# Two reciprocal roots on another engine, a load ahead of a store, and statistics behind low parts, in an attention and mixture-of-experts layer

## Time and profile before

| | |
|---|---|
| median of 3 runs | 2802.78 us (2802.04 to 2803.43) |
| the profiled execution, its own time | 2804.82 us |
| its span | 2803.1 us |
| TensorE busy | 2755.0 us, 98% of the span |
| VectorE busy | 2185.9 us, 78% |
| ScalarE busy | 1405.3 us, 50% |
| GpSimd busy | 637.9 us, 23% |
| mean granted clock of TensorE | 0.988 of full speed |
| on the chain that ended last | TensorE 89%, VectorE 4%, transfers 3% |

### The profile page before, as it was taken

How to read it: one execution, slowest core, us unless ns; L and a number is a source line. 1 busy time by engine, 2 the same in 40 slices (tenths; PEclk the granted TensorE clock), 3 DMA queues, 4 the chain that set the end, 5 groups by cost and what they waited for, 6 DMA issues and landing times.

```text
span 2803.1 us, 41819 instructions
## 1 busy us (share of the span) xinstructions
PE 2755.0 (98%) x13088; PEld 2287.4 (82%) x13088; DVE 2185.9 (78%) x3194; ACT 1405.3 (50%) x2495; POOL 637.9 (23%) x627
## 2 busy tenths in 40 slices
PE   8999999999999999999999999999999999999988
PEld 7888888888888888888888888888887878888867
DVE  5888888888888888888888888888888777433346
ACT  5555555566555555755555556555555321244424
POOL 2121211122222122221111213221211100266510
PEclk9999999999999999999999999999999889999999
DMA  3111111113111111221111113111110411478943
GB/s 117 38 35 38 34 37 34 34 34 116 34 37 35 34 34 38 64 84 37 34 34 34 34 36 110 34 37 34 34 42 27 138 48 41 136 229 252 246 135 138
DMA packets 209640, 193.53 MB, mean 69 GB/s; under 512 B 14620, under 2 KB 162076, under 8 KB 209552
## 3 DMA queue, kind: packets, MB, share of 16 engines
q1 hardware_dynamic: 199056, 180.47, 20.4%
q0 software_dynamic: 10496, 12.02, 2.2%
HBM read 166.41 MB, written 36.18 MB: 72 GB/s over the span
## 4 chain that ended last, share of the span: by engine, by line
PE 89%; DVE 4%; DMA 3%; issue 2%; ACT 1%; POOL 1%; SPq 0%; POOLq 0%; ACTq 0%; DVEq 0%
PE banks L1718 36%; PE banks L1733 24%; PE banks L1756 12%; PE banks L1640 4%; PE banks L1689 3%; PE banks L1649 3%; DMA acc_rows<-rows_b,who 2%; PE banks L1702 2%; PE banks L1743 2%; PE banks L1571 1%; DVE colsum L1277 0%; POOL acc_rows L686 0%; PE banks L1676 0%; PE banks L1596 0%; DVE neg_max L1262 0%
## 5 line engine op out<-in xcount | busy, mean ns | idle before, releaser
L1718 PE MATMUL banks<-xt,w_sb 128*128 (+1 forms) x4608 | 1108.6, 390 | 6.6 <-DVE xt L1356 6.5
L906 ACT ACTIVATE rows_a<-banks,neg_max 128x1024 f32<-128x1024 f32 x512 | 572.5, 1118 | 893.2 <-DVE neg_max L1262 892.8
L1718 PEld LDWEIGHTS banks<-xt,w_sb 128*128 128x128 f32 x4608 | 866.3, 188 | 187.2 <-POOL w_sb L625 6.5
L1262 DVE TENSOR_REDUCE neg_max<-banks 128x1 f32<-128x1024 f32 x512 | 626.0, 1223 | 285.9 <-PE banks L1733 283.1
L1733 PE MATMUL banks<-qk 128*128 128x512 f32 x3072 | 781.0, 390 | 3.2 <-ACT rows_a L906 3.0
L1733 PEld LDWEIGHTS banks<-qk 128*128 128x128 f32 x3072 | 576.9, 188 | 124.8 <-issue 3.4
L1277 DVE SCALAR_TENSOR_TENSOR colsum<-rows_a,inv,colsum 128x1024 f32<-128x1024 f32 x448 | 586.3, 1309 | 18.8 <-DVE inv L1269 1.5
L625 POOL TENSOR_TENSOR w_sb<-raws,w_sb 128x512 fp32r<-128x512 f32 x192 | 258.0, 1344 | 1201.6 <-ACT w_sb L860 1201.6
L1756 PE MATMUL banks<-wo_sb,val 128*128 128x512 f32 x1536 | 372.0, 391 | 1.2 <-DVE y_sb L1312 1.2
L1756 PEld LDWEIGHTS banks<-wo_sb,val 128*128 128x128 f32 x1536 | 285.9, 188 | 67.8 <-DVE y_sb L1312 8.0
L1640 PE MATMUL banks<-xt 128*128 128x512 f32 x768 | 194.7, 413 | 0.0
(11 more groups left out here) (184 smaller groups left out, 2262.5 us busy)
## 6 DMA issues: line engine op xcount, KB each, us to landing
raws<-in_w_qkv SPq DMA_DIRECT2D x192, 256.0 KB, 2.9
wo_raw<-in_w_o SPq DMA_DIRECT2D x64, 256.0 KB, 2.8
y_sb<-in_x SPq DMA_DIRECT2D x32, 256.0 KB, 4.2
raw_own<-in_w_gate SPq DMA_DIRECT2D x16, 512.0 KB
raw_own<-in_w_up SPq DMA_DIRECT2D x16, 512.0 KB
raw_own<-in_w_down SPq DMA_DIRECT2D x16, 512.0 KB
raws<-in_xT SPq DMA_DIRECT2D x25, 256.0 KB, 3.0
x_wide<-y_sb SPq DMA_DIRECT2D x24, 256.0 KB, 3.7
```

Source lines behind the costliest of these rows:

```text
L906: act.activation(ex[:, t % 2], p_s[:, t % 2], ACT.Exp, bias=neg_max[:, t % 2], accum_out=rowsum[:, t % 2]).then_inc(act_e, 1)
L1262: dve.tensor_reduce(neg_max[:, t % 2], p_s[:, t % 2], AX_X, ALU.max, negate=True)\
L1718: ins = pe.matmul(p_g[:, g % 2], w_sb[:, a, r, c], xt_part(batch_par, b, c, half * NB, NB), start=(c == 0 and (a, b) == PASSES[0]), stop=( ...
```

## The change

Three edits. The scale and shift of turns 6 and 7 are computed on GpSimd, by the `scale_x` that is there for the others; for turn 6 in front of three iotas, for turn 7 behind the store of turn 1's weights. `load_rows(5)` and its wait stand in front of `store_x(7)` on SyncE. `stats_o(0)` stands behind `lo_t(3, 0)` and `lo_t(3, 1)` on VectorE.

```diff
--- before.py
+++ after.py
@@ -576,9 +576,9 @@
         store_a(0)
         sp.wait_ge(out_a[2], 16)
         load_rows(4)
-        store_x(7)
         sp.wait_ge(pe_t, TT * 4)
         load_rows(5)
+        store_x(7)
         store_a(2)
         store_a(4)
         sp.wait_ge(out_a[2], 32)
@@ -713,6 +713,7 @@
             pool.wait_ge(act_s, 2 + h)
             pool.tensor_tensor(s_down[:, LO, two], s_raw[:, two], rounded(s_down[:, HI, two]),
                                ALU.subtract).then_inc(pool_s, 1)
+        scale_x(6)
         pool.iota(iota_s[:], [[1, C_SLOTS]], base=0, channel_multiplier=0,
                   allow_small_or_imprecise_dtypes=True).then_inc(pool_k, 1)
         pool.iota(names[:, :, 0], [[0, TURNS * TT * TOPK]], base=1, channel_multiplier=1,
@@ -723,6 +724,8 @@
         for c in range(TURNS):
             on_pool.wait_ge(dve_w, 2 * c + 2)
             pool.dma_start(rows_of(weights_of, c), dense[:, c % 2]).then_inc(out_w[c % 2], 16)
+            if c == 1:
+                scale_x(7)
 
         pool.wait_ge(pe_t, TT * 6)
         for q in range(2):
@@ -1081,12 +1084,6 @@
         tt, ts, stt = dve.tensor_tensor, dve.tensor_scalar, dve.scalar_tensor_tensor
         ro = Chain(dve, ro_c)
         link = Chain(dve, ln_c)
-
-        def scale_x(c):
-            on_dve.wait_ge(act_q, 2 * TT * (c + 1))
-            on_dve.wait_ge(act_ln, TT * (c - 1))
-            ln_rsqrt(dve, link, EPS, n_square[:, c % 2], small[:, 0], n_scale[:, c % 2], small[:, 2], 1.0 / D)
-            tt(n_shift[:, c % 2], n_mean[:, c % 2], n_scale[:, c % 2], ALU.mult).then_inc(scaled, 1)
 
         def stats_o(c, tiles=range(TT)):
             q, i = OUT_BUF[c], OUT_ORDER.index(c)
@@ -1390,7 +1387,6 @@
         choose_experts(0)
         lo_t(2, 2)
         lo_t(2, 3)
-        scale_x(6)
         weigh(0)
         choose_groups(1)
         add_shared(0, 0)
@@ -1429,8 +1425,6 @@
             for j in range(TT):
                 add_shared(u, j)
             collect(u)
-            if u == 2:
-                scale_x(7)
 
         add_logits(6)
         choose_groups(6)
@@ -1488,10 +1482,10 @@
             lo_hidden(n, f)
 
         share_step(5, 0)
-        stats_o(0)
         share_step(5, 1)
         lo_t(3, 0, True)
         lo_t(3, 1, True)
+        stats_o(0)
         share_step(5, 2)
         stats_o(2)
         share_step(5, 3)
```

## The result

| | kernel before | changed kernel |
|---|---|---|
| median of the first runs | 2802.41 us (4 runs, 2795.53 to 2803.43) | 2781.76 us (4 runs, 2779.92 to 2782.15) |
| its profiled execution | 2804.82 us | 2782.15 us |
| its span | 2803.1 us | 2780.4 us |
| mean granted clock | 0.988 | 0.992 |
| TensorE busy | 2755.0 us | 2746.6 us |

The ratio is 0.993, with a 95% interval of 0.9913 to 0.9947: faster, by 20.6 us (0.7%). The forecast was 2786.4 us, range 2782.8 to 2793.2, so the time came out 4.6 us under the forecast and 1.0 us under the range. The direction was right, the number was not.

The account below looks back on a forecast made before the run. TensorE, busy 98% of the span, was taken as the bound. Terms 0 + 0 + 5.7 + 0.9 + 9.8 = 16.4 us off 2804.8 gave 2788.4 for such an execution, 2786.4 us for the median; range 2782.8 to 2793.2.

Parts of the forecast that it names:

- Load ahead of the store: Routing, turn 5: TensorE's 3.72 us wait for rows_a and the low clock behind it go; 5.7 us gained (5.2 to 6.4).
- the clock: Routing, behind logits: the shift may remove or bring a clock drop; 0.9 us gained, bounds 4.4 gained to 2.7 lost.
- a drop that the forecast had among its bounds: Routing, behind turn 5's logits: a low clock may newly come there, costing 2.7 us.
- The drop behind turn 6's logits: Routing: product takes 8.28 us at clock 0.65 against 5.56 at full; a third of the 2.7 us taken as gain, 0.9.
- Roots: Scale and shift of turns 6 and 7 moved from VectorE to GpSimd: each worth 0 us.
- Statistics behind low parts: End of kernel: TensorE's 9.40 us wait goes, 12.2 us removed, 2.3 and 0.15 back; net 9.8 us (8.1 to 10.2).
- The new wait of 2.3 us before `down(5)`: End: down(5) would wait for the low part of part 2, still behind stats_o(0); 2.3 us lost.
- A low clock inside `down(5)`: End: clock drop after the new 2.3 us wait, about 1.7 us lost; none taken in the forecast.
- Neither moves against the other: End: load of accumulated rows and TensorE's work keep their spacing, so stats_o(0) still ends at 2702.09, where the next product starts.
- Swallowed: Rival: accumulating transfers paced by memory, so 5.7 and 0.9 us are lost, 2793.0 us; chance 0.15, including load still late.
- Locked out: Rival: VectorE's two-input SBUF instructions stretch GpSimd's root beyond 25 us; 2805 us, slower than before; chance 0.02.
- the forecast's limit: Routing, turn 7: the root may end until about 25 us after ScalarE's sums (2257.5) without cost.

Follow-up runs that it names:

- the four unmoved rows: Profiles of four kernels with stats_o(0) where it was, first load of accumulated rows about 11 us behind gate_up(5, 0): lengths 119.6, 120.3, 120.3, 120.0 us.
- before_delay: Kernel before plus 24 small dependent GpSimd products in front of the last pair of accumulating transfers: 2799.46 us (10 runs), ratio 1.0000.
- later: Changed kernel with stats_o(0) moved behind share_step(5, 2) and stats_o(2) behind share_step(5, 3): 2780.53 us (7 runs), ratio 0.9951 to the kernel before.
- load_only: Kernel before with only load_rows(5) and its wait put in front of store_x(7): 2791.25 us (11 runs), ratio 0.9975.
- roots_only: Kernel before with only the two roots (turns 6 and 7) moved to GpSimd: 2791.12 us (12 runs), ratio 0.9979.
- load_tail: Kernel before with the load ahead of the store and the statistics behind the low parts, both roots left on VectorE: 2779.75 us (6 runs), ratio 0.9944.
- after_again: The changed kernel, unchanged, timed again in a job with the kernel before: 2782.32 us (11 runs), ratio 0.9948.
- after_delay: Changed kernel plus 24 small dependent GpSimd products in front of the last pair of accumulating transfers: 2786.74 us (5 runs), ratio 0.9961 to the kernel before.
- the two kernels with the delay: Changed kernel with 24 GpSimd products ahead of the last accumulating transfers, 2786.74 us; the same with both statistics one place further down, 2782.51 us.

## Why the prediction was wrong

**The step that failed: "2804.8 - 16.4 = 2788.4 for such an execution, 2786.4 for the median".** The 16.4 is not the part that failed. The changed kernel is at 2781.9 as the median of its 15 runs, the kernel before at 2798.3 as the median of its 106 runs in the five jobs: 16.4 apart, or 15.2 (10.6 to 18.7, from the interval of the ratio) within the one job that has both. That it agrees to a tenth is luck: the interval is 8 us wide, and several terms behind it were off in both directions, as shown below. What did not hold is the 2802.8 it was taken from. Its three runs lay within 1.4 us of each other and were read as the kernel's time; of the 106 only 13 are over 2802.0, and they reach from 2786.4 to 2805.9. With 2798.3 in its place, 4.5 us less, the same sum gives 2781.9. The range was built from the terms of the change alone and held nothing for the base.

**The profile of before was one execution of many, too.** Against that of after it differs by 22.7 us, because three things fell badly in it and better in the other: the low clock in turn 1's logits (2.9 us, in front of the edits), the expert stage (2.0 us) and the late transfers (lag 14.8 against 11.0). The last is 4.2 us by the lengths 124.3 and 120.1, the latter the mean of the four unmoved rows with a lag near 11. Without the three, 13.6 of the 22.7 are left. The expert stage takes 248.9 to 252.4 us in the profiles without a delay of the transfers, in no order of the edits. Turn 1's logits take 6.87 or 6.88 us in eleven of the 19 profiles and 3.66 to 3.94 in eight. Both occur where the edits in front of them are the same (before 6.88 and before_delay 3.85; `later` 6.87 and after 3.94), so an edit is not needed for it. Seven of the eight, however, are among the ten with both roots on GpSimd; whether these make the short time more frequent stays open.

**Load ahead of the store, 5.7, and the clock, 0.9.** Together 6.6; the starts of the experts differ by 5.6 on average, and the load alone is worth 7.0 in time. The wait is gone in every profile with this edit or the root of turn 7, and the product behind it runs at full clock. But the price was that of one execution: of the five profiles that have the wait, two (3.72 and 3.40 us) show the low clock behind it, with transposes of 1.97 us, and three (1.66 to 1.93 us) do not:

```profile
2294.55 1.09 PE L1571 MATMUL banks<-ident,rows_a 128*128 128x128 f32 x8 [1.66 <-DMA rows_a<-x_wide]
```

In these three less than 2 us hang on the load, not 6.4. What makes up the rest of load_only's 7.0 us (4.2 to 10.1) no run here shows. VectorE limits the gain as forecast where the clock in front of turn 6's second pair of transposes is full. TensorE then waits for the low part, in load_only:

```profile
2317.41 1.23 PE L1571 MATMUL banks<-ident,y_sb 128*128 128x128 f32 x8 [0.27 <-DVE xt L1122]
```

Seven of the fourteen profiles without the wait for rows_a have this, 0.26 to 0.36 us. The other seven, the changed kernel's two among them, have a low clock behind turn 5's logits in its place, a drop that the forecast had among its bounds and the profile of before did not show:

```profile
2307.53 1.95 PE L1565 MATMUL banks<-ident,y_sb 128*128 128x128 f32 x8
```

From turn 5's transposes to that second pair of turn 6 it is 26.21 us there and 25.14 in load_only, so the drop costs about 1.1 us here. The drop behind turn 6's logits, taken as a third gone, is still there in the changed kernel (7.74 us for 8.28). In time the term of the clock cannot be told from chance; starts differ by up to 8.3 us among profiles with the wait and by 8.6 among those without.

**Roots, 0 and 0.** Right in the sum, wrong in the reason. The forecast brought `write_x(7)` from 2284.34 to about 2273.4 (measured: 2268.74, and 2272.60 in roots_only), and stopped there. Behind it in SyncE's order stands store_x(7), and behind that the load TensorE waits for. So the root of turn 7 alone is worth 6.2 us (1.1 to 8.4). In the whole change no worth of it shows, since the load no longer stands behind that store (load_tail against the changed kernel). Whether the root of turn 6 is worth anything by itself stays open.

**Statistics behind low parts, 9.8.** By the lengths: 124.3 (forecast from) to 116.5, 115.9 or 114.6 with a late lag, so 7.8 to 9.7; and 120.1 to 111.9 = 8.2 with an early one. The new wait of 2.3 us before `down(5)`, taken as certain, is 2.61, 2.25 and 2.16 where the lag is near 15, and nothing where it is 11, which is the commoner case (5 of the 7 profiles with this edit and no delay). Then, however, the wait removed is only about 6 as well, so the two mistakes nearly cancel. A low clock inside `down(5)`, priced at 1.7 and not taken, came in after_again (1.77) and in after_delay.

**"Neither moves against the other"** (load of accumulated rows and gate_up(5, 0)) was false: between executions of one kernel they move by 4 us. It is the assumption behind the certain wait, and part of what the 2802.8 did not hold: an execution of the kernel before with an early end is 4.2 us shorter.

**The rivals.** Swallowed: no; the stage's lead reached the end (10.3 us early at gate_up(5, 0) in the changed kernel's profile), and the transfers moved with it. Locked out: the roots took 4.5 us (turn 6) and 6.0 us (turn 7), and even 20.6 us of delay, which brought the root to the forecast's limit, cost TensorE no wait. The 1.05 us of one 0.20 us instruction in that root lie beside VectorE's 1.22 us product of two SBUF tiles, 2256.20 to 2257.42: as in the earlier trace rows. The Trainium skill, "SBUF — State Buffer", Who interferes with whom, states that such a pair lock each other out; this trace agrees. The root's other two long instructions (0.75 us from 2255.59, 0.66 us from 2257.84) also lie beside VectorE products of two SBUF tiles (0.69 us from 2255.59, 0.68 us from 2257.76). The price was about 1.5 us of hidden time.

**Faster versions.** The load and the statistics alone (load_tail, 2779.75) are at least as good as the whole change, with a smaller edit. The later statistics add what the late executions lose (4.2 us between the two kernels with the delay, by 4 and 5 runs whose intervals overlap), and nothing measurable otherwise. No run separates these from the whole change.

## What to carry to other kernels

Set the base of a forecast by the spread of many executions, or widen the range by it: three equal times do not show that a kernel has one time. When an edit makes a step early, follow every queue in which that step stands in front of something, because two edits may remove one wait. And a wait that depends on a transfer's end should be priced at both ends that this transfer shows, not at the one in the trace at hand; a second trace of the unchanged kernel would have shown the other end.

## What the runs showed of the hardware that was not expected

- One program, same chip, one job: 2788.1 to 2805.9 us in 29 runs, 0.6%. The clock goes along: in that job the four runs with a mean granted clock of 0.987 average 2803.8 us, the nine with 0.988 2800.7, the three with 0.992 2789.5.
- The same 32 thin matmuls take 6.88 us in one execution and 3.94 in another, also where no edit stands in front of them (before 6.88, before_delay 3.85).
- A chain of accumulating transfers ends 11 or 15 us behind the same instruction of TensorE, by chance of the execution: in 11 of the 16 profiles in which nothing holds the transfers back on purpose at 11.0 to 11.6 us, in four at 14.8 to 15.1, in one at 13.4. One transfer of the chain that takes 7.28 us instead of some 4, and ScalarE's wait for its buffer (3.94 us against none), carry it in after_again.
